# VectorE's small operations dealt out singly between scans and products in a Mamba, cross-attention and expert layer

## The reference, cut to what matters

```python
def _layernorm(x): return (x - mean(x)) / sqrt(var(x) + 1e-5)
# Mamba: 512 channels, 16 states each
def step(h, inp):
    d_t, b_t, c_t, u_t = inp
    h = h * exp(d_t[:, :, None] * A) + (d_t * u_t)[:, :, None] * b_t[:, None, :]
    return h, einsum("bdn,bn->bd", h, c_t)
# delta = softplus(...); y = (ys + u * D) * silu(z); out = y @ out_proj.T
x = _layernorm(x + mamba(x))
# cross-attention: two norms inside, relu feed-forward of 1024
x = _layernorm(x + xattn(x, ctx))
# experts: top 8 of 160
probs = sigmoid(x @ router_w.T + expert_bias)
top_w, top_idx = top_k(probs, 8)
top_w = 2.5 * top_w / (sum(top_w) + 1e-9)
x = _layernorm(x + sum_e top_w[e] * (silu(x @ w_gate[e].T) @ w_down[e].T) + shared(x))
```

## Time and profile before

| | |
|---|---|
| median of 3 runs | 1081.67 us (1078.8 to 1085.27) |
| the profiled execution | 1086.31 us, of which its span of instructions is 1084.6 us |
| mean granted TensorE clock | 0.942 |
| busy: PE, PEld, DVE, ACT, POOL | 890.3, 740.6, 818.1, 632.0, 746.6 us |
| the 128 scans (L1748) and their products (L1755) on DVE | 293.2 and 156.0 us |
| the 128 inflows (L467) on POOL | 300.2 us |
| scan 0 of turns 3, 4, 5, 6 and 7 starts at | 253.0, 329.1, 406.1, 482.9, 559.8 us |

### The profile page before, as it was taken

One profiled execution on the slowest core, in us unless ns is written; L12 is line 12 of the kernel. 1 busy time (PEld: TensorE's weight loads), 2 busy tenths in 40 slices (PEclk: granted clock), 3 DMA queues, 4 the chain that ended last, 5 costly groups with the idle time before them and its releaser, 6 DMA issues. The chain is left out here.

```text
span 1084.6 us, 17808 instructions
## 1 busy us (share of the span) xinstructions
PE 890.3 (82%) x5032; PEld 740.6 (68%) x5032; DVE 818.1 (75%) x1595; ACT 632.0 (58%) x1578; POOL 746.6 (69%) x649
## 2 busy tenths in 40 slices
PE   6778878998998989989949888609998989989475
PEld 4566666786776877867847767508887878778354
DVE  0689899899999999999999956735655555555176
ACT  4786685876976966957846544205555555455100
POOL 1554667757879989889899976555777777777400
PEclk9888899999999999999989899958999999999698
DMA  7492834924134143151061112449998989997495
GB/s 246 175 301 104 267 106 156 345 77 128 47 104 139 49 140 102 54 190 70 22 204 54 52 54 93 150 154 325 321 295 268 295 261 300 285 298 239 186 344 208
DMA packets 118060, 195.48 MB, mean 180 GB/s; under 512 B 17476, under 2 KB 82914, under 8 KB 115522
## 3 DMA queue, kind: packets, MB, share of 16 engines
q1 hardware_dynamic: 79410, 134.28, 38.4%
q0 software_dynamic: 16592, 35.46, 9.0%
q10 hardware_dynamic: 21952, 24.51, 7.1%
HBM read 155.21 MB, written 75.64 MB: 213 GB/s over the span
## 5 line engine op out<-in xcount | busy, mean ns | idle before, releaser
L467 POOL TENSOR_TENSOR inf_all<-bc_all,du 128x1024 f32<-128x1024 f32 x128 | 300.2, 2362 | 58.5 <-DVEq L1746 44.4
L1748 DVE TENSOR_TENSOR_SCAN DA<-DA,inf_all 128x1024 f32<-128x1024 f32 x128 | 293.2, 2291 | 16.7 <-ACT DA L737 10.8
L2294 POOL DMA_INDIRECT yp_dram<-u,sz x216 | 212.8, 985 | 77.5 <-issue 45.8
L737 ACT ACTIVATE DA<-dl,a_neg 128x255 f32<-128x255 f32 x512 | 212.0, 462 | 0.2
L2361 ACT ACTIVATE u<-DA,sz 128x256 f32<-128x256 f32 x216 | 102.4, 474 | 116.7 <-DMA yp_dram<-u,sz 84.5
L1755 DVE TENSOR_TENSOR hb_all<-DA,bc_all 128x1024 f32<-128x1024 f32 x128 | 156.0, 1218 | 8.3 <-DVE DA L1748 0.5
L2329 PE MATMUL DA<-hb_all,sz 128*128 128x256 f32 x432 | 136.8, 399 | 19.9 <-ACT sz L2354 19.5
L2322 PE MATMUL DA<-sz,hb_all 128*128 128x128 f32 x864 | 133.9, 278 | 3.0 <-issue 3.0
L1172 PE MATMUL Y<-ident,hb_all 128*128 128x128 f32 x1024 | 134.0, 281 | 0.8 <-DVE hb_all L1755 0.8
L1172 PEld LDWEIGHTS Y<-ident,hb_all 128*128 128x128 f32 x1024 | 122.6, 146 | 8.6 <-issue 2.1
L2322 PEld LDWEIGHTS DA<-sz,hb_all 128*128 128x128 f32 x864 | 115.4, 195 | 3.4 <-issue 3.4
(11 more groups left out here) (491 smaller groups left out, 1679.4 us busy)
## 6 DMA issues: line engine op xcount, KB each, us to landing
hb_all<-in_w_moe SPq DMA_DIRECT2D x216, 256.0 KB
bc_all<-bc_dram SPq DMA_DIRECT2D x32, 1024.0 KB, 5.8
inf_all<-xe_dram SPq DMA_DIRECT2D x216, 140.0 KB
bc_all<-yp_dram SPq DMA_DIRECT2D x16, 1024.0 KB, 7.1
xe_dram<-zeros ACTq DMA_DIRECT2D x2, 7420.0 KB, 25.8
xe_dram<-zeros ACTq DMA_DIRECT2D x1, 7560.0 KB, 27.1
yp_dram<-u,sz POOLq DMA_INDIRECT x216
w<-in_w SPq DMA_DIRECT2D x2, 1024.0 KB, 7.0
```

The source lines that it names most:

```text
L467: g.tensor_tensor(inf[(b * NTAU + t) % NI][:, :, :], bc[gr][:, 0, :, :], du[p][:, c, :].unsqueeze(1).to_broadcast([P, SG, T]), ALU.mult).t ...
L737: ins = s.activation(da[:, n, 1:T], dl[p][:, c, 1:T], ACT.Exp, scale=a_neg[:, c, st:st + 1])
L1748: v.tensor_tensor_scan(da[:, :], da[:, :], inf[(b * NTAU + t) % NI][:, :, :].rearrange("p n t -> p (n t)"), 0.0, ALU.mult, ALU.add).then_i ...
L2294: g.indirect_dma_start(yp_dram, bass.IndirectOffsetOnAxis(ap=pid[:, half * UNROLL + s_:half * UNROLL + s_ + 1], axis=0), ys[s_][:, :], Non ...
```

## The change: what it does

On VectorE the block of `weigh` and `address` is cut into single operations, which stand from scan 2 to product 7. The AGGREGATEs of the four norms are separated from their STATS by other work. `softplus` moves from behind product 11 to between scan 11 and product 11. `ln3` and `ln1` are interleaved. On ScalarE `chosen_exp` moves ahead, directly behind `mask`. No operation is added or taken away, and GpSimd's, TensorE's and SyncE's orders stay. The tail behind turn 7 still uses `weigh` whole.

```diff
@@ ScalarE, turn @@
                 if exists(s - 3):
                     mask(s - 3)
+                    chosen_exp(s - 3)
...
-                if exists(s - 3):
-                    chosen_exp(s - 3)
@@ VectorE @@
-            def moments(i, src, b):
+            def spread(i, src):
                 for q in range(QT):
                     v.bn_stats(stats[:, i, q, :], src[:, q, :]).then_inc(stat1[i].sem, 1)
+
+            def gathered(i, b):
                 dve.wait_ge(stat1[i].sem, stat1[i].at(b, QT))
                 dve.sem_inc(tick, 1)
                 for q in range(QT):
                     ins = v.bn_aggr(mv[:, i, q, :], stats[:, i, q, :])
                 ins.then_inc(stat2[i].sem, 1)
...
@@ VectorE, turn @@
                     scan(s, 2)
+                if exists(s - 3):
+                    found(s - 3, key)
+                if exists(s):
                     outflow(s, 2)
+                if exists(s - 3):
+                    odds(s - 3)
+                if exists(s):
                     scan(s, 3)
                 if exists(s - 3):
                     lanes(s - 3)
+                    chances(s - 3)
                 if exists(s):
                     outflow(s, 3)
+                if exists(s - 3):
+                    total(s - 3)
+                if exists(s):
                     scan(s, 4)
                 if exists(s - 1):
-                    ln0(s - 1, 1 - p)
+                    ln0(s - 1)
+                if exists(s - 3):
+                    placed(s - 3)
+                if exists(s - 1):
+                    gathered(0, s - 1)
+                if exists(s - 3):
+                    scaled(s - 3)
                 if exists(s):
                     outflow(s, 4)
+                if exists(s - 3):
+                    inverse(s - 3)
+                    counted(s - 3)
+                if exists(s):
                     scan(s, 5)
                     y(s, p, 0)
+                if exists(s - 3):
+                    slots(s - 3)
+                    gates_row(s - 3, x2e[1 - p])
+                if exists(s):
                     outflow(s, 5)
+                    scan(s, 6)
                 if exists(s - 3):
-                    weigh(s - 3, x2e[1 - p], key)
+                    names_row(s - 3, x2e[1 - p])
                     address(s - 3)
                 if exists(s):
-                    scan(s, 6)
                     outflow(s, 6)
                     scan(s, 7)
+                if exists(s - 3):
+                    counted_on(s - 3)
...
                     scan(s, 11)
+                if exists(s + 1):
+                    softplus(s + 1, 1 - p)
+                if exists(s):
                     outflow(s, 11)
                 if exists(s + 1):
-                    softplus(s + 1, 1 - p)
                     softplus_max(s + 1, 1 - p)
+                if exists(s - 2):
+                    ln2(s - 2)
+                if exists(s + 1):
                     delta(s + 1, 1 - p)
                 if exists(s - 2):
-                    ln2(s - 2, p)
+                    gathered(2, s - 2)
...
                     delta_u(s + 1, 1 - p)
+                if exists(s - 1):
+                    ln1_sum(s - 1)
+                if exists(s - 2):
+                    ln3_sum(s - 2, p)
+                if exists(s - 1):
+                    ln1_merge(s - 1)
                 if exists(s - 2):
                     ln3(s - 2, p)
                 if exists(s - 1):
                     ln1(s - 1)
+                if exists(s - 2):
+                    gathered(3, s - 2)
+                if exists(s - 1):
+                    gathered(1, s - 1)
```

More of the change, by code:

```diff
@@ L1777, in moments, with ln0 @@
                 ins.then_inc(stat2[i].sem, 1)
-            def ln0(b, p):
+            def ln0(b):
                 dve.wait_ge(out_f.sem, out_f.at(b, 1))
-                moments(0, pair(QA), b)
+                spread(0, pair(QA))
             def softmax(b):
@@ L1838, in choose_last, with found, odds, chances @@
                 v.tensor_scalar(msk_b[:, :, :], rep[:, :, :], PICKED, None, ALU.is_ge).then_inc(mask_d.sem, 1)
+            def found(b, lg):
+                for q in range(QT):
+                    v.max_index(ti[:, q, :], top[:, q, :], lg[:, q, :]).then_inc(pick.sem, 1)
+            def odds(b):
+                dve.wait_ge(lg_e.sem, lg_e.at(b, 1))
+                v.tensor_scalar(pr[:, :, :], pr[:, :, :], 1.0, None, ALU.add).then_inc(pick.sem, 1)
+            def chances(b):
+                dve.wait_ge(pick.sem, pick.at(b, 7))
+                v.reciprocal(pr[:, :, :], pr[:, :, :]).then_inc(pick.sem, 1)
+            def total(b):
+                dve.wait_ge(pick.sem, pick.at(b, 8))
+                v.tensor_reduce(psm[:, :], pr[:, :, :], AX.X, ALU.add).then_inc(pick.sem, 1)
+            def scaled(b):
+                dve.wait_ge(pick.sem, pick.at(b, 9))
+                v.tensor_scalar(psm[:, :], psm[:, :], 1e-9, 0.4, ALU.add, ALU.mult).then_inc(pick.sem, 1)
+            def inverse(b):
+                dve.wait_ge(pick.sem, pick.at(b, 10))
+                v.reciprocal(psm[:, :], psm[:, :]).then_inc(pick.sem, 1)
+            def gates_row(b, rows_):
+                dve.wait_ge(pick.sem, pick.at(b, 11))
+                v.tensor_tensor(rows_[:, :, G0:G0 + TOPK], pr[:, :, :],
+                                psm[:, :].unsqueeze(2).to_broadcast([P, QT, TOPK]), ALU.mult).then_inc(pick.sem, 1)
+            def names_row(b, rows_):
+                w8 = QT * TOPK
+                dve.wait_ge(pick.sem, pick.at(b, 6))
+                v.tensor_copy(rows_[:, :, E0:E0 + TOPK], ti[:, :, :]).then_inc(pick.sem, 1)
+                v.tensor_copy(rows_[:, :, P0:], pairs[:, bass.ds(b * w8, w8)].rearrange("p (q k) -> p q k", q=QT)).then_inc(pick.sem, 1)
             def weigh(b, rows_, lg):
@@ L1864, in lanes, with placed, counted, slots @@
                                 home[:, :].unsqueeze(1).to_broadcast([P, QT, NE]), ALU.add).then_inc(cum_c.sem, 1)
-            def address(b):
+            def placed(b):
                 dve.wait_ge(cum_c.sem, cum_c.at(b, 1))
                 v.scalar_tensor_tensor(rep[:, :, :], rep[:, :, :], PICKED, cum[:, :, :], ALU.is_ge, ALU.mult).then_inc(addr.sem, 1)
+            def counted(b):
                 v.tensor_tensor(m_sum[:, :], m_sum[:, :], msk_b[:, 0, :], ALU.add).then_inc(addr.sem, 1)
+            def slots(b):
                 dve.wait_ge(addr.sem, addr.at(b, 1))
```

19 lines of the change are left out of this document (13 added, 6 removed).

## The result

The changed kernel took 1114.73 us in the median of 4 runs (1111.54 to 1118.37), the kernel before 1082.28 beside it; the ratio is 1.0295, with a 95% interval from 1.0276 to 1.0314. The direction was right, the size was not: 1093.7 was forecast, with a range up to 1104. The profiled execution took 1111.54 us (span 1109.8).

What follows compares the result with a forecast made beforehand. A closed loop through VectorE and GpSimd was taken as the bound: +2.8 us in each of three loops (8.4), +0.5 in turn 3, +1 in turns 0 to 2, +2 in turn 7, together +12 on 1081.67: 1093.7 us, range 1077 to 1104.

Steps and rivals of the forecast that it cites:

- the term for `odds`: Wait of VectorE's odds among GpSimd's inflows 3 to 5; taken at 0.4 us, between 0 and 2.33.
- link 1: Scan 14 of one turn to norm 0's AGGREGATEs in the next, 27.26 us before; forecast +1.3 us (0.9 to 3.3).
- the port is lost again and again: Rival: the next inflow wins, so odds or gates_row waits 2.3 us more in five turns; 1105 us, chance 0.08.
- Link 3: GpSimd from the root of norm 0 to the end of inflow 13, 31.21 us before; forecast 0, at worst +0.5.
- the loop: Closed chain through VectorE and GpSimd from scan 14 to scan 14, 76.72 us; forecast +2.8 us in each of three.
- The rival in which VectorE pays in full: VectorE's order sets the turn, so five turns with routing save 2.9 us each; 1067 us, chance 0.14.
- Link 4: End of inflow 13, through softplus, to norm 2's AGGREGATEs, 4.55 us before; product 11 enters it, forecast +0.8 us.
- Link 6: Root of norm 2, through the roots of norms 3 and 1, to scan 14, 13.29 us before; forecast +0.7 us.
- Turns 0 to 2: Wait for the logarithm, 0.8 us at most, partly lost in existing waits; forecast +1 us together (0 to 2.4).
- Turn 3: Inflow 13 is in time; VectorE saves some 1.9 us but pays at softplus, link 6 and gates_row; forecast +0.5 us.
- Turn 7: Of the loop only links 1 and 6 lengthen in this turn; forecast +2 us.
- the signs named beforehand: Turns of 79 to 80 us; GpSimd waiting over 1 us for norm 0; scan 14 waiting 1 us or more; others.

Runs made afterwards that it cites:

- that run: Changed kernel with gates_row and counted_on moved behind scan 6 into a run of scatters, odds left in place; ratio to the kernel before 1.0263.
- the two parts alone: Kernel before with only softplus put between scan 11 and product 11, ratio 1.0062; kernel before with only norms 3 and 1 interleaved, ratio 1.0056.
- without the stands: Changed kernel with odds ahead of product 1 and gates_row and counted_on behind scan 6; median 1094.19 us, ratio to the kernel before 1.0116.
- `odds` alone: Kernel before with only odds moved behind product 2 and chosen_exp ahead, directly behind mask; ratio 1.0129, 14 us more.

## Why the prediction was wrong

**The step that failed** is the term for `odds` in link 1: "its wait lies between 0 and one whole inflow (2.33), and by the CAST, the nearest row, it lasts to the end of the inflow it meets. I take 0.4." The place was seen (inflows 3 to 5, back to back), the size was not. It measured 4.0 in turn 5 and 18.9 in the five turns together, where the sum had 0.4 a turn. The bound was drawn from two rows, the CAST and `softplus`; both meet the last inflow of a run, with a scatter behind it, so the end of the inflow and GpSimd's next gap are the same moment in them. These are the scatters, on GpSimd in the kernel before:

```profile
432.20 1.07 POOL L527 DMA_INDIRECT xe_dram<-x2e,ad_i  x1 [0.18 <-issue]
...
457.16 1.80 POOL L527 DMA_INDIRECT xe_dram<-x2e,ad_i  x1 [0.17 <-issue]
```

The two rows could not tell the two readings apart, and the milder one was taken for a bound. In the changed kernel it held in turn 3 alone (2.27), and not in turns 4 to 7. The Trainium skill ("SBUF — State Buffer", section "Who interferes with whom") has the engine that comes second blocked for the whole instruction of the other; the runs here show it blocked for a whole chain of them in most cases (4.15 us against 0.73 with a scatter put into the chain; 24 stands of 29), and the measurement decides. The rival "the port is lost again and again" had the mechanism, at 2.3 us and 8 in 100; it lost the port twice more, to inflow 5 and to `base2_`.

**Link 1 without it**: +0.9 was worked out, +0.64 measured in turn 5 with the three operations clear of inflows (0.44 to 0.93 in turns 3 to 7). **Link 3** was right, and it is the strongest test of the loop: `gates_row` and `counted_on` cost VectorE 4.3 us a turn there, and the stretch stayed at 31.2. The rival in which VectorE pays in full falls with that run, and with the two parts alone that save VectorE time and lose. **Link 4**: +0.8 forecast, 1.12 measured, 0.75 where VectorE is early enough that inflow 13 and not the logarithm decides. **Link 6**: +0.7 forecast, 0.68 measured. **Turns 0 to 2**: +1 forecast, 2.09 measured (scan 14 of turn 2 starts at 247.31 instead of 245.22). **Turn 3**: +0.5 forecast, 2.84 measured, 0.34 without the stands. **Turn 7**: +2 forecast, 5.82 measured, 0.82 without them.

The parts add up within what can be measured: some 14 us for `odds` alone, 6.7 for `softplus` and 6 for the norms, 27 in all; the rest of link 1 in five turns is another 3 to 4, against 32 for the whole change. That gaps on VectorE are saved is seen in the rows of the changed kernel (product 2 begins 0.09 before the search for indices ends, 429.37 against 429.46), but this saved time lies ahead of waits.

Of the signs named beforehand, GpSimd's waits for norms 0 and 3 (5.10 and 0.90), the wait of scan 14 (1.82) and the idle time before `softplus` (0.91) came; turns of 79 to 80 us came only without the stands; scan 10 did not begin to wait, since VectorE did not run ahead.

## What to carry to other kernels

Read for each small operation on VectorE what GpSimd runs at that moment, and behind it until its next gap: an instruction of 0.16 us placed into a run of back-to-back products cost the rest of the run here in most turns, if it was of a kind that waits for them at all. An upper bound for a wait must come from a row where the candidate causes end at different moments. And before gaps are covered, ask what ends the stretch: time saved ahead of a wait is only waited for longer, while work put ahead of what another engine waits for costs its full length.

## What the runs showed of the hardware that was not expected

- A VectorE operation that waits for a running inflow is mostly not let in between instructions of GpSimd that follow each other without a gap (24 stands of 29). Those shown here end 0.03 to 0.10 us behind the last instruction ahead of a gap: one of 0.16 to 0.17 us ahead of a scatter, or one in which GpSimd waits.
- Not every small operation waits. Additions and scalings (TENSOR_SCALAR) over 16 and 2 elements, a CAST and products of two operands stood; the search for indices took 0.32 us inside inflow 4 (429.14), and a RECIPROCAL over the same 16 elements as `odds` took 0.23 inside an inflow (431.22, the inflow from 429.88 to 432.25), no more than behind one (0.25).
- It goes the other way too: the small operations of a root took up to 1.68 us on GpSimd instead of 0.72 beside `softplus` and its followers.
- A scatter is mostly, but not always, a safe cover. Of some 250 small operations of the block that start inside a scatter in the twelve traces, all but 14 take 0.3 us at most; 10 stand to about the scatter's end, and 4 into the inflow behind it (`scaled` three times, started 0.04 to 0.05 us ahead of the scatter's end, and `odds` with its 5.34, started 0.41 into one of 1.01). In the changed kernel a CAST that started 0.48 into another (451.64 against 451.16) took 0.16, and the COPY behind it 0.40 instead of 0.11. What decides that stays open.
